# A GpSimd memset with a wait behind each in-loop scatter of a graph kernel

## The reference, cut to what matters

```python
feat_all = einsum('ni,rhid->rnhd', inputs, conv_weights)      # 8 relations, 4 heads of 64
feat_src_e = feat_all[edge_type, edge_src]
...
ex = exp(leaky_relu(el + er) - m[edge_dst])                    # m: largest of the destination's edges
denom = segment_sum(ex, edge_dst)
h = segment_sum((ex / denom[edge_dst])[..., None] * feat_src_e, edge_dst)
```

## Time and profile before

| what | value |
|---|---|
| median of 3 runs | 3268.11 us (3263.8 to 3269.29) |
| span of the profiled execution | 3494.0 us |
| mean granted TensorE clock, profiled execution | 0.904 |
| busy share of the span: PE, DVE, ACT, POOL | 84%, 53%, 36%, 29% |
| edge loop from its first scatter to its last, profiled | 601.7 to 1557.1 us |

### The profile page before, as it was taken

The page is one execution under the profiler, slowest core; times in us unless marked ns, Lnnn a source line. Parts: engine busy times, 40 slices in busy tenths (PEclk is TensorE's granted clock), DMA queues, the critical chain, the costliest instruction groups (busy, mean ns, idle before and its releaser), DMA issues.

```text
span 3494.0 us, 48240 instructions
## 1 busy us (share of the span) xinstructions
PE 2934.6 (84%) x15020; PEld 1947.6 (56%) x15084; DVE 1869.1 (53%) x5320; ACT 1260.7 (36%) x3665; POOL 1013.3 (29%) x1048
## 2 busy tenths in 40 slices
PE   2799936888888888889268799989999999999998
PEld 2444416777777777778142444445555555545545
DVE  6578745666666665556250543334555555532334
ACT  1122235666666666668020220004444444420000
POOL 2144465666666666665710000000000000000000
PEclk6699968898999899999559699999999999999999
DMA  8966643222222222221128243330000000022232
GB/s 250 363 180 194 183 125 86 70 73 74 71 74 71 73 74 72 74 66 28 31 71 301 82 119 103 101 118 6 3 6 6 6 3 6 23 76 79 78 101 80
DMA packets 245032, 314.35 MB, mean 90 GB/s; under 512 B 121467, under 2 KB 168484, under 8 KB 240740
## 3 DMA queue, kind: packets, MB, share of 16 engines
q1 hardware_dynamic: 191412, 175.79, 17.8%
q0 software_dynamic: 49104, 104.11, 10.2%
q10 hardware_dynamic: 4320, 31.95, 2.3%
HBM read 234.14 MB, written 77.59 MB: 89 GB/s over the span
## 4 chain that ended last, share of the span: by engine, by line
PE 57%; DVE 15%; issue 11%; ACT 7%; another core or an unknown queue 4%; DVEq 3%; DMA 3%; SPq 0%; ACTq 0%
PE PS L1153 15%; PE PS L998 14%; PE PS L964 7%; PE PS L939 5%; PE PS L977 5%; PE PS L822 4%; ACT BG L653 3%; DMA BG<-a_d 3%; DVE BG L1703 2%; DVEq L1582 2%; DVE OHB L1430 1%; ACT SL L736 1%; DVE AL L1790 1%; DVE SUMS L1411 1%
## 5 line engine op out<-in xcount | busy, mean ns | idle before, releaser
L1567 DVE TENSOR_TENSOR SUMS<-SUMS,PS 128x640 f32 x500 | 409.2, 818 | 374.2 <-PE PS L939 220.7
L532 POOL DMA_INDIRECT BG<-feat_d,IDXST x500 | 485.9, 972 | 337.9 <-PE PS L939 157.4
L523 POOL DMA_INDIRECT a_d<-VAL,IDXS x499 | 492.3, 987 | 314.3 <-DVE VAL L1424 133.2
L1153 PE MATMUL PS<-BG,SL 128*128 128x512 f32 (+1 forms) x1440 | 539.1, 530 | 12.0 <-ACT SL L736 12.0
L653 ACT ACTIVATE BG<-BG,SL 128x64 f32<-128x64 f32 x2000 | 513.4, 336 | 0.0
L1153 PEld LDWEIGHTS PS<-BG,SL 128*128 128x128 f32 x1440 | 277.0, 195 | 251.7 <-issue 222.4
L564 POOL MEMSET BG<- 128x7680 f32 x1 | 6.5, 6501 | 1327.3 <-DVE MV L1834 1327.3
L964 PE MATMUL PS<-W1A,X 65*128 65x256 f32 x1000 | 295.2, 421 | 81.8 <-ACT X L627 60.4
L939 PE MATMUL PS<-OHB,BG 128*128 128x128 f32 x2000 | 357.2, 305 | 0.2
L977 PE MATMUL PS<-OHB,X 128*128 128x128 f32 x2000 | 337.5, 295 | 23.1 <-issue 22.6
L977 PEld LDWEIGHTS PS<-OHB,X 128*128 128x128 f32 x2000 | 306.7, 208 | 40.0 <-issue 25.1
(11 more groups left out here) (298 smaller groups left out, 4093.0 us busy)
## 6 DMA issues: line engine op xcount, KB each, us to landing
BG<-a_d SPq DMA_DIRECT2D x171, 256.0 KB, 4.2
AL<-a_d SPq DMA_DIRECT2D x137, 256.0 KB, 2.6
a_d<-BG POOLq DMA_DIRECT2D x30, 1088.0 KB, 40.2
feat_d<-SUMS ACTq DMA_DIRECT2D x30, 1040.0 KB
BG<-rel_d SPq DMA_DIRECT2D x100, 160.0 KB
X<-in_edge_attr_dram SPq DMA_DIRECT2D x124, 128.0 KB
SUMS<-a_d SPq DMA_DIRECT2D x52, 256.0 KB, 2.6
SL<-key_d SPq DMA_DIRECT2D x50, 192.0 KB
```

The source lines that it names most:

```text
L523: pool.indirect_dma_start(a_d.rearrange("n (w o) -> (n w) o", o=1), bass.IndirectOffsetOnAxis(ap=IDXS[:, t:t + 1], axis=0), VAL[:, t:t + 1 ...
L532: pool.indirect_dma_start(RING[:, t // NB % 3, t % NB, :], None, feat_d.rearrange("n (r d) -> (n r) d", r=R), bass.IndirectOffsetOnAxis(ap ...
L1153: last = pe.matmul(PS[:, to + q, 0:width], lhs[:, i, c, :], w[:, c, q * width:(q + 1) * width], start=(c == 0), stop=(c == kc - 1))
L1567: add = tt(a, a, SUM_AT[n % 3].rearrange("p (a n) -> p a n", a=5), ALU.add)
```

## The change

A block of X is named that nothing else uses at that time, 32 partitions of 448 float32. Behind each of the 207 in-loop scatters POOL writes zeros into it and waits for that instruction's completion before its next instruction, which is a gather. Between two such memsets POOL issues two gathers and one scatter. The first 85 gathers, the 150 early scatters and the 142 scatters behind the last gather are as before.

```diff
+        BREATH = XF[32:64, 896:1344]
...
                 if t >= LEAD and (t - LEAD + 1) * 1 // 2 > (t - LEAD) * 1 // 2:
                     scatter_late(counted)
                     counted += 1
+                    step(pool.memset(BREATH, 0.0))
```

## The result

The kernel with the change takes 3379.05 us (3369.17 to 3380.04, 4 runs), the kernel before in the same session 3268.70 (3263.80 to 3269.42): a ratio of 1.0339, interval 1.0324 to 1.0355. It is slower by 110 us; forecast were 97. The record of the change spans 3376.7 us, 117 less than the record of before, though its runs are 110 longer.

The account below looks back on a forecast made before the run. The prediction took POOL's pace in the edge loop, 3.80 us for a pair of tiles, to bound the kernel. 207 memsets at 0.47 us add 97.3 us to 3268.1, giving 3365 us (+3.0%), range 3220 to 3460.

Parts of the forecast that it names:

- The stops are not in the runs: Engine stops in the profiled execution, mostly in the edge loop, are made by recording and largely absent from the runs.
- The tally of the stops: 161.9 us in the loop, 38.4 at the first gathers, 12.0 behind the last scatter: 212.3 of 225.9 us excess.
- POOL is the pace, 3.80 us for a pair: In the runs' edge loop POOL sets the pace, 3.80 us for a pair of tiles, with PE waiting for rows.
- PE's pace, 3.33 us: PE needs 1.67 us a tile, 3.33 us for two, read at the edge loop's end.
- The memset's price, 0.47 us for a pair: Behind each in-loop scatter a pair grows by 0.47 us, the memset's own length, the wait's 0.15 us overlapping with starts.
- The bounds, 0.32 and 0.92: Least and most growth of an in-loop pair in us, by how starts and wait overlap: 3334 to 3459 us.
- The sum: 207 in-loop memsets x 0.47 us = 97.3 us on 3268.1, giving 3365 us, +3.0%.
- PE late once in a batch: In the edge loop PE is idle once in a batch until its rows have landed; no size given.
- The scatters behind the last gather: Behind the loop's last gather 58 scatters are let through with PE's tiles, 84 follow the last tile; all shift along.
- "Hidden": Rival: the memset runs beside the scatter's DMA on POOL, adding nothing (3268 us) or 31 us (3299); chance 0.16.
- "Other pacing": Rival: DVE, ACT or clock hold pairs at 4.0 us, 3324; or POOL's completion comes late, 3485; counted to the forecast.
- "Faster": Rival: stops are in the runs and the gap lets PE's signals through, 76 to 113 us gained, 3155 to 3192; chance 0.20.

Follow-up runs that it names:

- before, recorded again: The kernel before, unchanged, recorded a second time: one run of 3260.16 us, span 3258.4 us.
- the run with every third gather: The kernel before with an in-loop scatter behind every third gather in place of every second, the rest behind the loop: 3300.24 us, ratio 1.0113.
- the traces with one and with 896 elements: The change with its memset writing one or 896 float32 per partition in place of 448: 3299.22 us (ratio 1.0100) and 3444.71 us (1.0556).

## Why the prediction was right, and where not

- **The stops are not in the runs.** Right, and the sign hung on it: the same kernel, recorded again, has neither the stops nor the long span. Wrong in the reason: "recording makes them" would put them into each record, and none of the eleven others has a span more than 12 us off its runs' median. So the span of the change did fall while its runs got longer, but because the record of before was the odd one, and not because the gap lets signals through. The Trainium skill's rule on overflow (NOTIFIC — the notification-queue block, "Overflow: three behaviours, one of which stalls the engine") fits one record that was held up, but no row here shows such a stall as its cause.
- **The tally of the stops.** Its 212.3 us came within 13.6 of the excess in part by luck. Against before, recorded again, the first record is longer by 22 us from the first gather to the first in-loop scatter (38.4 in the tally), by 159 in the loop (161.9), by 20 from there to the last scatter (not in the tally) and by 33 from the last scatter to SP's load (12.0).
- **POOL is the pace, 3.80 us for a pair.** Right: 3.81 in the clean record, 3.865 in the mean, with 1.9 us of waiting ahead of the gathers.
- **PE's pace, 3.33 us.** Too fast: 3.58 (2 x 1.79) where edges are counted.'s stretch was the loop's end. The sum did not need it, since POOL is the slower in both, but the margin was 0.2 us and not 0.47 (3.80 - 3.33), and in the run with every third gather it was gone.
- **The memset's price, 0.47 us for a pair.** Right: 0.49 for the memset, + 0.27 - 0.30 = 0.46 to 0.47 from scatter to scatter. The bounds, 0.32 and 0.92, held it well. No row had shown the two starts; the prediction let them cancel, and they do but for 0.03, which is in part luck. In the mean a pair grew by 0.521. The other 0.05, 11 us in all, are slips: 8 us are the nine late starts, which stand at the same nine gathers in the traces with one and with 896 elements and at none where the gather does not wait; nearly all the rest is gathers that last longer, 406.7 us for 402.9. What makes the nine stays open.
- **The sum.** 97 for 110: 96 at 0.466, 11 of slips, 2 of the last scatter's landing (20.0 us for 17.9) make 109.4, and that is the whole distance in POOL's chain. The term that came out too small is 207 x 0.47, which held for pairs where nothing slips.
- **PE late once in a batch.** Right: DVE waits for a batch's rows 18 times, 107.5 us, where it was 8 times and 26.9 us, and PE stops behind it once in a batch, 84 us in all.
- **The scatters behind the last gather.** Wrong: none of the 142 waits for a tile, neither before nor after; they go at POOL's own pace to 1671.16 and layer two waits for them. The number is the same, since all of it shifts.
- **The rivals.** "Hidden" falls: in the trace the memset starts at the scatter's end, and, whatever spans on POOL are worth, a longer memset makes the pair and the run longer by its own length. The rule under "Instruction dispatch" in the GPSIMD Engine Reference of the Trainium skill, that a core goes on when its own share is done, would let it start earlier; in this trace it does not, and only 0.11 us of the wait is saved when none is made. "Other pacing" (0.20 us covered) has no room: POOL had 1.9 us of waiting. Its other half, a completion that comes 1.2 us late, fits nine of the 207 gathers and not the rest. "Faster" falls with the stops.

## What to carry to other kernels

First ask whether a record is typical: where its span is several per cent off the runs, record again before reading any wait in it. On an engine that no one holds up, a small instruction costs its own length plus the difference of the starts around it, times its count, and here a tenth more in slips, however long the other engines are idle; the same instruction where its engine waits anyway cost 0.3 to 7 us for 150 of them. And a pace is read in the stretch whose work it shall stand for, since the tiles at a loop's end may do less, and it is divided by what that engine did there: TensorE sums more tiles than POOL gathers while it works off a lag.

## What was not expected of the hardware

One record of a kernel was 235.6 us longer than another of the same kernel (3494.0 and 3258.4). In it TensorE, VectorE and ScalarE stopped together, for 21.8 to 23.1 us at the longest, while POOL went on with a run of indirect DMAs such as the other record has without any such stop. In the traces a memset behind an indirect DMA on POOL starts at once, where an indirect DMA needs 0.30 us; an indirect DMA behind a memset starts 0.16 us after it, and 0.27 if it waits for its completion, except for nine of 207 that start some 1.2 us after it. One element in 32 partitions takes 0.12 us, 448 take 0.49 and 896 take 0.87. Where SP waits for the last scatter alone, its load starts 17.8 to 20.0 us after that scatter does.
